# State space beside the first attention: decays in a PSUM bank, sums by accumulating transfers, products with C on POOL

## What is computed

```python
def step(state, xs):                       # over 256 positions, for 4 batches
    d_t, B_t, C_t, u_t = xs
    dA = jnp.exp(d_t[..., None] * A)       # [256 channels, 16 states]
    state = state * dA + (d_t * u_t)[..., None] * B_t[:, None, :]
    y_t = jnp.einsum('ben,bn->be', state, C_t)
    return (state, y_t)
# attention: softmax(q k^T / sqrt(8)) v, all heads, no mask
```

## Time and profile before

| | us |
|---|---|
| median of 3 runs | 2946.87 (2944.28 to 2950.98) |
| profiled execution | 2950.47 |
| its span | 2949.1 |

### The profile page before, as it was taken

How to read it: one execution, slowest core, us unless ns; L and a number is a source line. 1 busy time by engine, 2 the same in 40 slices (tenths; PEclk the granted TensorE clock), 3 DMA queues, 4 the chain that set the end, 5 groups by cost and what they waited for, 6 DMA issues and landing times. The chain is left out here.

```text
span 2949.1 us, 35916 instructions
## 1 busy us (share of the span) xinstructions
PE 2178.2 (74%) x13065; PEld 1501.3 (51%) x13112; DVE 1756.7 (60%) x3211; ACT 1060.0 (36%) x2152; POOL 926.1 (31%) x785
## 2 busy tenths in 40 slices
PE   6467635999938888755125999978999788677737
PEld 2233314777627787633013444456888645434424
DVE  6999774444445555546886544544555553695477
ACT  3245415545514444321222244433344344103522
POOL 3876602655635655512430000012222200000020
PEclk8656767999969999977557898998999999897969
DMA  3222100000014444210000000020000000000000
GB/s 129 63 59 59 30 20 26 17 21 15 5 67 159 152 154 162 90 39 36 7 0 35 3 3 2 3 94 1 1 1 1 1 1 2 22 22 1 2 34 15
DMA packets 48431, 114.60 MB, mean 39 GB/s; under 512 B 5472, under 2 KB 18144, under 8 KB 46976
## 3 DMA queue, kind: packets, MB, share of 16 engines
q1 hardware_dynamic: 46720, 108.10, 11.5%
q0 software_dynamic: 1536, 4.20, 0.4%
HBM read 100.09 MB, written 11.14 MB: 38 GB/s over the span
## 5 line engine op out<-in xcount | busy, mean ns | idle before, releaser
L1656 POOL TENSOR_SCALAR l0f_probs<-l0f_probs,l0f_tot 128x128 f32<-128x128 f32 (+1 forms) x256 | 190.4, 763 | 133.0 <-DVE l0f_tot L1610 132.9
L1150 DVE TENSOR_REDUCE l2a_a_max<-ps 128x6 f32<-128x768 f32 x128 | 119.4, 955 | 117.1 <-PE ps L1003 116.4
L1878 PE MATMUL ps<-l0f_xh,l0f_wh 128*128 128x256 f32 x480 | 147.4, 307 | 49.8 <-DVE l1x_dBu L593 28.2
L2821 POOL TENSOR_TENSOR l2x_probs<-l2x_probs,l2x_rc 128x512 f32<-128x512 f32 x64 | 66.5, 1039 | 268.6 <-DVE l2x_rc L2736 268.6
L1993 POOL TENSOR_TENSOR l0f_wl<-l0f_raw,l0f_wh 128x1024 fp32r<-128x1024 f32 x60 | 141.8, 2375 | 17.4 <-ACT l0f_wh L1918 17.4
L1879 PE MATMUL ps<-l0f_xl,l0f_wh 128*128 128x256 f32 x480 | 139.1, 290 | 0.0
L1880 PE MATMUL ps<-l0f_xh,l0f_wl 128*128 128x256 f32 x480 | 139.1, 290 | 0.0
L1540 ACT ACTIVATE l0f_probs<-ps,l0f_neg 128x128 f32<-128x128 f32 (+1 forms) x256 | 104.6, 426 | 87.3 <-DVE l0f_neg L1600 87.3
L1878 PEld LDWEIGHTS ps<-l0f_xh,l0f_wh 128*128 128x128 f32 x480 | 94.9, 198 | 57.6 <-issue 31.7
L871 POOL TENSOR_TENSOR l0x_y<-l0x_y,l0x_hc 128x512 f32<-128x512 f32 x64 | 106.2, 1677 | 55.7 <-DVE l0x_hc L853 55.7
L618 POOL TENSOR_TENSOR l1x_y<-l1x_y,l1x_hc 128x512 f32<-128x512 f32 x64 | 80.7, 1282 | 125.2 <-DVE l1x_hc L609 125.2
(11 more groups left out here) (751 smaller groups left out, 6009.2 us busy)
## 6 DMA issues: line engine op xcount, KB each, us to landing
l0f_raw<-in_e_l0f SPq DMA_DIRECT2D x60, 512.0 KB, 3.8
l0x_bc<-scratch_bc SPq DMA_DIRECT2D x32, 512.0 KB, 4.8
l0f_raw_d<-in_e_l0f SPq DMA_DIRECT2D x60, 256.0 KB, 3.7
scratch_rows<-zero SPq DMA_DIRECT2D x1, 3840.0 KB, 18.8
l0f_xb<-scratch_rows SPq DMA_DIRECT2D x15, 256.0 KB, 4.2
scratch_results<-l0f_yb SPq DMA_DIRECT2D x15, 256.0 KB, 4.5
l0f_slab<-in_g_l0f SPq DMA_DIRECT2D x8, 448.0 KB, 3.6
l1f_raw<-in_w_l1f SPq DMA_DIRECT2D x1, 3072.0 KB, 10.1
```

The costliest lines, as they stand in the source:

```text
L1150: dve.tensor_reduce(M[:, 2 * half:2 * half + 2, j, :], src.rearrange("p a (c n) -> p a c n", c=NB_), AX.X, ALU.max).then_inc(*unit_max.tick())
L1656: last = pool.tensor_scalar(pr[:, u % 3, a, r], pr[:, u % 3, a, r], tot[:, u % 3, qt, a:a + 1], None, ALU.mult)
L1878: pe.matmul(out, hi, xh[:, j % 2, c, :], start=c == 0, stop=False)
```

## The change

- The decays of a half go to PSUM bank 3 instead of SBUF, a single buffer for both halves in turn: ACT makes half 0 of step i at the end of slot 3i+2 and half 1 at slot 3i+3, each after the scan of the half before; DVE scans half 0 at slot 3i+3, half 1 at slot 3i+4. The products follow at slot 3i+5.
- The products of steps 5 to 25 (`POOLED`) are made by POOL, the others by DVE as before.
- y += hc is no longer a POOL addition: POOL issues one accumulating transfer per step, SBUF to SBUF, both halves at once (512 KB). hc[i % 2] is reused once the transfer of step i − 2 has landed. After the last step POOL waits for all.
- Bank 3 is lost to the ring. Units take banks 0 and 1, one after another (no second buffer); turns, rows, weigh and back take bank 2 in their own order. So that they fit into one bank, turns are of two tiles (five a pass, in slots 2, 3, 6, 7 and 10) instead of up to four, and the two parts of a weigh or back stand side by side in the bank.
- Two semaphores are merged with others of the same kernel (a_exp into a_chain, zeroed into tables).

The other attentions (`scan` is None) keep their ring.

```diff
-    STEPS, RING = 32, 3
+
+    STEPS, RING, POOLED = 32, 3, range(5, 26)
...
@@ -798,14 +799,17 @@
-    def steps(self, cx):
+    def steps(self, cx, bank):
-        self.dA, self.dBu, self.hc = (sb(n, [P, 2, 2, 2, S]) for n in ("dA", "dBu", "hc"))
+        self.dA = bank.rearrange("p (b s) -> p b s", s=S)
+        self.dBu, self.hc = (sb(n, [P, 2, 2, 2, S]) for n in ("dBu", "hc"))
         self.h = sb("h", [P, 2, 2, S])
         self.fetched = [k.sig(f"scan_rows{i}", 16) for i in range(self.RING)]
-        self.decay, self.drive, self.state, self.seen, self.summed = (k.sig("scan_" + n) for n in ("decay", "drive", "state", "seen", "sum"))
-        k.dve.memset(self.dA[:, :, :, :, 0:1], 0.0).then_inc(*k.sig("v").tick())
+        self.decay, self.drive, self.state, self.seen = (k.sig("scan_" + n) for n in ("decay", "drive", "state", "seen"))
+        self.summed = [k.sig(f"scan_added{i}", 16) for i in range(2)]
+        self.late = k.sig("scan_late")
+        k.dve.memset(self.dA[:, :, 0:1], 0.0).then_inc(*k.sig("v").tick())
         k.act.wait_ge(*k.sig("v").now())
 
     def row(self, t):
@@ -813,6 +817,13 @@
 
     def half(self, i):
         return slice(2 * (i % 2), 2 * (i % 2) + 2)
+
+    def by_pool(self, i):
+
+        return 2 * sum(x in self.POOLED for x in range(i))
+
+    def by_dve(self, i):
+        return 2 * i - self.by_pool(i)
 
     def sp(self, g):
         k, (i, r) = self.k, (g // 3 + 2, g % 3)
@@ -822,35 +833,48 @@
                 k.sp.wait_ge(*self.bc_out.now())
             if i >= self.RING:
                 k.sp.wait_ge(*self.drive(2 * (i - self.RING) + 2))
-                k.sp.wait_ge(*self.seen(2 * (i - self.RING) + 2))
+                k.sp.wait_ge(*self.seen(self.by_dve(i - self.RING + 1)))
+                k.sp.wait_ge(*self.late(self.by_pool(i - self.RING + 1)))
             src = k.bc_rows.rearrange("(z n) t -> n z t", z=2)[n:n + 1, :, hf * HALF:(hf + 1) * HALF]
             k.sp.dma_start(self.bc[:, i % self.RING, :, :], src.to_broadcast([P, 2, HALF])).then_inc(*self.fetched[i % self.RING].tick())
 
     def act(self, g):
+
         k, (i, r) = self.k, divmod(g, 3)
-        if r == 0 and i < self.STEPS:
-            for d in range(2):
-                if i >= 2:
-                    k.act.wait_ge(*self.state(2 * (i - 2) + d + 1))
-                k.act.activation(self.dA[:, i % 2, d, :, 1:S], self.dt[:, d, self.half(i), 1:S], ACT.Exp,
-                                 scale=self.An[:, d, i // 2:i // 2 + 1]).then_inc(*self.decay.tick())
+        if r == 2 and i < self.STEPS:
+            self.decays(i, 0)
+        if r == 0 and 0 <= i - 1 < self.STEPS:
+            self.decays(i - 1, 1)
+
+    def decays(self, i, d):
+        k = self.k
+        if i or d:
+            k.act.wait_ge(*self.state(2 * i + d))
+        k.act.activation(self.dA[:, :, 1:S], self.dt[:, d, self.half(i), 1:S], ACT.Exp, scale=self.An[:, d, i // 2:i // 2 + 1]).then_inc(*self.decay.tick())
 
     def dve(self, g):
         k, (i, r) = self.k, (g // 3 - 1, g % 3)
-        if r == 0 and 0 <= i < self.STEPS:
-            for d in range(2):
-                k.dve.wait_ge(*self.decay(2 * i + d + 1))
-                k.dve.wait_ge(*self.drive(2 * i + d + 1))
-                if i:
-                    k.dve.wait_ge(*self.seen(2 * (i - 1) + d + 1))
-                k.dve.tensor_tensor_scan(self.row(self.h[:, d]), self.row(self.dA[:, i % 2, d]), self.row(self.dBu[:, i % 2, d]), 0.0,
-                                         ALU.mult, ALU.add).then_inc(*self.state.tick())
-        if r == 1 and 0 <= i < self.STEPS:
-            for d in range(2):
+        if r < 2 and 0 <= i < self.STEPS:
+            k.dve.wait_ge(*self.decay(2 * i + r + 1))
+            k.dve.wait_ge(*self.drive(2 * i + r + 1))
+            if i:
+                k.dve.wait_ge(*self.seen(self.by_dve(i)))
+                k.dve.wait_ge(*self.late(self.by_pool(i)))
+            k.dve.tensor_tensor_scan(self.row(self.h[:, r]), self.row(self.dA), self.row(self.dBu[:, i % 2, r]), 0.0,
+                                     ALU.mult, ALU.add).then_inc(*self.state.tick())
+        if r == 2 and 0 <= i < self.STEPS:
+            for d in range(0 if i in self.POOLED else 2):
                 k.dve.wait_ge(*self.state(2 * i + d + 1))
-                if i >= 2:
-                    k.dve.wait_ge(*self.summed(2 * (i - 2) + d + 1))
-                k.dve.tensor_tensor(self.row(self.hc[:, i % 2, d]), self.row(self.h[:, d]), self.bc[:, i % self.RING, 1, :], ALU.mult).then_inc(*self.seen.tick())
+                self.settled(k.dve, i - 2)
+                self.weighted(k.dve, i, d).then_inc(*self.seen.tick())
+
+    def weighted(self, eng, i, d):
+        return eng.tensor_tensor(self.row(self.hc[:, i % 2, d]), self.row(self.h[:, d]), self.bc[:, i % self.RING, 1, :], ALU.mult)
+
+    def settled(self, eng, i):
+
+        if i >= 0:
+            eng.wait_ge(*self.summed[i % 2](i // 2 + 1))
 
     def pool(self, g):
         k, (i, r) = self.k, divmod(g, 3)
@@ -863,12 +887,18 @@
                                      ALU.mult).then_inc(*self.drive.tick())
         i -= 1
         if r == 2 and 0 <= i < self.STEPS:
-            for d in range(2):
-                yd = self.row(self.y[:, d, self.half(i)])
-                k.pool.wait_ge(*self.seen(2 * i + d + 1))
-                if i >= 2:
-                    k.pool.wait_ge(*self.summed(2 * (i - 2) + d + 1))
-                k.pool.tensor_tensor(yd, yd, self.row(self.hc[:, i % 2, d]), ALU.add).then_inc(*self.summed.tick())
+            for d in range(2) if i in self.POOLED else ():
+                k.pool.wait_ge(*self.state(2 * i + d + 1))
+                self.settled(k.pool, i - 2)
+                self.weighted(k.pool, i, d).then_inc(*self.late.tick())
+            k.pool.wait_ge(*self.seen(self.by_dve(i + 1)))
+            k.pool.wait_ge(*self.late(self.by_pool(i + 1)))
+            self.settled(k.pool, i - 2)
+            k.pool.dma_start(self.y[:, :, self.half(i)].rearrange("p d b s -> p d (b s)"), self.hc[:, i % 2].rearrange("p d b s -> p d (b s)"),
+                             accum_op=ALU.add).then_inc(*self.summed[i % 2].tick())
+            if i == self.STEPS - 1:
+                for s in self.summed:
+                    k.pool.wait_ge(*s.now())
 
@@ -906,7 +936,8 @@
     H, K, NO, SPO, NU, NB_ = hs.H, 3 * hs.hd, len(hs.octets), len(hs.parts), len(hs.units), 3 if hs.causal else 2
     NC, LEAD = NO * SPO, 3 if PAR == 4 else 2
     scale = 1.0 / math.sqrt(hd)
-    turns = [("k", x, min(4, KJ - x)) for x in range(0, KJ, 4)] + [("q", x, 4) for x in range(0, NJ, 4)]
+    TM = 2 if scan else 4
+    turns = [("k", x, min(TM, KJ - x)) for x in range(0, KJ, TM)] + [("q", x, TM) for x in range(0, NJ, TM)]
     NT_ = len(turns)
 
...
     def turns_at(s):
+        if scan:
+            return [i for i in range(NT_) if s == 4 * (i // 2) + 2 + i % 2]
...
-    uses, place = [], {}
+    uses, place = {"units": [], "others": []}, {}
+    units, others = uses["units"], uses["others"] if scan else uses["units"]
     for it, s in [divmod(i, NC) for i in range((NB2 + 2) * NC + LEAD + 4)]:
         n = (it - 2) * NC + s - LEAD
         if it < NB2:
-            uses += [("turn", it, i) for i in turns_at(s)]
+            others += [("turn", it, i) for i in turns_at(s)]
         if 0 <= it - 1 < NB2:
-            uses += [("unit", it - 1, u) for u in units_at(s)] + ([("rows", it - 1, 0)] if s == NC - 2 else [])
-        uses += [("weigh", O, 0) for O in octet_at(n, 1)] + [("back", O, 0) for O in octet_at(n, 2)]
-    for i, u in enumerate(uses):
-        place[u] = i
+            units += [("unit", it - 1, u) for u in units_at(s)]
+            others += [("rows", it - 1, 0)] if s == NC - 2 else []
+        others += [("weigh", O, 0) for O in octet_at(n, 1)] + [("back", O, 0) for O in octet_at(n, 2)]
+    for kind in uses:
+        for i, u in enumerate(uses[kind]):
+            place[u] = kind, i
+    SLOTS = 1 if scan else 2
 
-        return ps[:, 2 * (place[u] % 2):2 * (place[u] % 2) + 2, :]
+        kind, i = place[u]
+        if kind == "others":
+            return ps[:, 2:3, :]
+        return ps[:, 2 * (i % SLOTS):2 * (i % SLOTS) + 2, :]
+    def pair(*u):
+        banks = ring(*u)
+        return banks[:, 0, :].rearrange("p (a s) -> p a s", a=2) if scan else banks[:, :, 0:S]
 
     def ring_free(*u):
-        if place[u] < 2:
+        ring_, at = place[u]
+        if at < SLOTS:
             return vc(0)
-        kind, b, i = uses[place[u] - 2]
+        kind, b, i = uses[ring_][at - SLOTS]
...
                 b, (m, half) = O // NO, hs.octets[O % NO]
-                banks = ring("weigh", O, 0)
+                banks = pair("weigh", O, 0)
                 pe.wait_ge(*weighed(SPO * (O + 1)))
                 pe.wait_ge(*ring_free("weigh", O, 0))
                 for a in range(2):
@@ -1045,11 +1093,12 @@
                         q0 = P if causal and kt else 0
                         for g in range(4):
```

(19 more changed lines are left out.)

## The result

| | median us | runs | ratio to before, 95% |
|---|---|---|---|
| before | 2948.80 | 2942.67 to 2956.69 (19) | |
| after | 2933.86 | 2926.10 to 2941.67 (19) | 0.9949 [0.9941, 0.9957] |

The profiled execution of after took 2936.3 us, with a span of 2935.0. The medians differ by 14.9 us, or 0.5%, where 16 us were forecast; the interval of the ratio leaves no doubt that after is the faster.

A forecast was written before the change was run, and what follows sets the result against it. The prediction took DVE and POOL to be taking turns at something shared in the first attention's stage. Gains of 11.3 + 3 + 2 + 0 = 16 us would bring the median from 2946.9 to 2931, range 2914 to 2951.

The forecast's parts named there:

- Scans at 1.19 us: State-space scans on DVE: with one input in PSUM a scan takes 1.19 us, bounds 1.17 and today's 1.80.
- Rival (d): Scans: the PSUM input frees nothing, DVE and POOL still take turns; 7 us gained in all, 2940; chance 0.08.
- Start: Steps 0 to 4, before the first maximum: a step goes from 7.62 to 4.8 us, four periods gain 11.3.
- First pass: First pass of row maxima: 39 us instead of 41.9, 3 gained.
- Scoring passes: Three passes that also score and weigh: 49.2 us each against 49.9, 2 gained; bounds 4.5 lost to 29 gained.
- rival (b): Scoring passes: single banks cost more, a pass takes 55 us, 15 lost over three; 2948; chance 0.16.
- rival (a): Passes: the PE clock rises as idle time shrinks, 14 us more gained, 2917, at most 2904; chance 0.15.
- Landing 5 us: Accumulating transfers: each 512 KB lands in 5 us, between 2.7 and 9.6, hidden except for the last.
- Rival (c): Accumulating transfers land slowly: at 14 us the kernel is 16 slower, 2963; slower from about 12.5; chance 0.11.
- End: Stage end after the passes: steps of 7.0 us instead of 7.65 gain 3.9, the tail takes back 4.2: 0.
- part 4: Smaller PSUM ring, the change's cost: units have one double bank; turns, rows, weigh and back share bank 2.
- parts 1, 2 and 3: In order: decays in PSUM; sums by accumulating transfers instead of POOL additions; products of steps 5 to 25 on POOL.

The follow-up runs named there:

- last_sum_dve: The changed kernel with the last step's two additions made by DVE, the last accumulating transfer being that of step 30: 2930.02 us, 0.9941 of before.
- weigh_split: The changed kernel with the next slot's unit issued on PE between the two halves of a weigh: 2946.33 us, 0.9972 of before.
- psum_only: The kernel before with only the decays in PSUM and the smaller ring this needs; additions on POOL, products on DVE: 2936.06 us, 0.9939 of before.
- sums_pool: The changed kernel with the accumulating transfers turned back into 64 POOL additions: 2925.04 us, 0.9916 of before; repeated on another chip, 2925.12 us, 0.9919.

## Why the prediction was right, and where its steps were not

The time (a median of 2933.9 against 2931), the stage's gain (16.8 against 16) and the central mechanism held: one input of the scan in PSUM, and DVE and POOL no longer take turns over the scans. That the total came within 1 us is luck in part. The four stretches of the sum missed by −2.9, +2.0, −1.8 and +3.1 us. Step by step:

**Scans at 1.19 us**: 1.217. Rival (d), that the PSUM input frees nothing, is out: scans stay at 1.22 beside the drives. The closed chain of exp and scan appeared as priced (0.76 us of wait for the second scan of a step in the start) and ACT's exponents did not suffer (1016 ns in the mean, 1023 before).

**Start, 11.3 forecast, 8.4 measured.** The first scans of steps 0 to 4 start at 65.15, 71.42, 76.91, 82.15 and 87.31, so four periods took 22.2 us, not 4 × 4.8 = 19.2. The term that was mis-sized is the products: 1.3 us for two, measured 1.84 to 2.13 from step 1 on. They still have two SBUF inputs, and the drives that run from 83.01 to 85.95 hold them up from 85.27 on (1.28 + 0.6); the prediction took them as free of POOL. That makes a step 5.2, not 4.8. Step 0 alone is over by 1.5, since its second scan waits 2.44 us for ACT; in last_sum_dve, with the same code there, it waits 1.33. Three smaller things nearly cancel: before took 29.8 us for its four periods and not 4 × 7.62 = 30.5, the first scan comes 0.6 later than before's 64.57, and from the first scan of step 4 to the first maximum there are 4.2 us instead of 5.6, which gives 1.4 back though the split of k (L1191) takes 2.07 beside a pair of drives and waits 0.97 for ACT ahead of that.

**First pass, 3 forecast, 5.0 measured**; 39 us were priced, 36.9 came. The PE clock stood at 0.73 in it, against 0.58 before, where the price was made at the low level. last_sum_dve runs the same code there at a clock of 0.59 and takes 38.7, as priced, and weigh_split at 0.63 takes 38.6. So the 2 us came with the clock of this execution. The start of last_sum_dve was shorter by 1.4, so that its pass was handed over only 0.4 later.

**Scoring passes, 2 forecast, 0.2 measured**, the sum of two misses. The clock: taken at 20% of the way up, it was at 0.67, 0.63 and 0.66, 31% in the mean, which by the sum gives 51.4 − 0.31 × 11.2 = 47.9 us a pass. Measured were 49.8. So the octets took 1.9 us a pass more than priced: rival (b)'s side, in the place it named, weigh slots and the shared bank (nine waits, 18.5 us, and weigh_split's chain). A part of rival (a) paid for a part of rival (b). The mean hides that single passes differ: 48.9, 54.8 and 45.7 us, so that two of them lie outside the 46 to 52 that the prediction named as its sign, and one just under the 55 that would have refuted it. Before they differed as much (50.4, 53.2, 46.0). The forecast of DVE's waits, 35 to 50 us "most in weigh slots", met 38.7, of which about half are there.

**Landing 5 us**: 7.2 in the median. The size depended on what ran beside. With 27 of the transfers a fetch of B and C was issued within 0.8 us, and they took 7.0 to 8.6 us. The one at 282.76, its nearest fetch 1.2 us later, took 6.1. The four without a fetch within 2.8 us (180.45, 306.80, 312.68, 320.05) took 5.3, 5.2, 5.0 and 5.0. The one that counts is the last, and it took the 5 that were forecast. The others were free: in the start, where they took 7.4 to 7.9, the product that needs the buffer again starts 8.25 to 8.48 us after the issue (77.02 to 85.27), so that less than 1 us was left, and no product waited for one. Rival (c) needed over 12.5.

**End, 0 forecast, 3.1 gained.** Both terms were off. The tail costs 2.9 (last_sum_dve) and not 4.2. From the last product's end, 319.35, to PE it took 7.7 us, where before took 2.9, so it grew by 4.8; but attention itself ends only 3.6 us after the last transfer's issue and would have held PE until 324.1 anyway. The steps gave 52.4 − 46.4 = 6.0, not 3.9.

**Products on POOL**: the prediction gave them no term of their own in the sum, "worth only what is DVE's turn in part 4". They are worth 5 to 8 us in the stage.

What the prediction did not see is how the parts overlap. It describes parts 1, 2 and 3 as three reliefs, one beside the other. Measured by stage ends, part 1 with its ring is worth 13.7 us (psum_only); part 2 gains 4.4 without it and costs 2 to 5 with it; part 3 gains 5 to 8: 13.7 − 4.7 + 7.8 = 16.8. The sum came out right because it was made over stretches of the stage with all parts in place; read as a statement on the parts, it would have been wrong for part 2.

## What to carry to other kernels

Where two engines stretch each other, ask of each pair that overlaps in time whether both use the shared read, and move one input of the instruction that meets it most: one PSUM operand of 64 scans was worth 32 us, while taking 106 us of additions off the other engine was worth 4 to 7. A second remedy for the same collision is to be priced with the first in place, for it may have nothing left to remove. And a wait that is moved off the head of a queue (units behind a weigh) should be followed to the next consumer in the same queue before it is counted as a gain.

## What the runs showed of the hardware

An accumulating transfer of 512 KB within SBUF took 5.0/7.2/8.6 us to land (minimum, median, maximum), 5.0 to 5.3 in the four cases without a load of the same size issued within 2.8 us, 7.0 to 8.6 in the 27 with one within 0.8 us. Such a load took 5.2 in the median, 4.8 in the kernel before. The issue held POOL for 1.2 us. The Trainium skill, "DMA: Bandwidth & Descriptors", section "Anatomy of one DMA", gives about 2.0 us plus the bytes at 436 GB/s, by which a landing would take 3.2, an estimate; the shortest measured is 5.0, and the measurement decides. A scan beside the issue was not stretched (1.23 us), beside two drives it took 2.95.

The code behind the stage, the same in all kernels, took 2597 to 2611 us in the profiled executions. In the eleven executions of sums_pool the eight near 2924 us had a mean PE clock of 0.845 to 0.848, the three near 2931 to 2934 one of 0.841 or 0.842. Why one kernel lands more often on the shorter side, which would make up most of sums_pool's 9 us, was not settled.
